# Filler products in front of each piece of maxima in a two-attention, two-mixture block

## The chip, the cores and the metric

The kernel runs on one core of one Trainium2 chip. The metric is the time of one launch in device microseconds (us). Three runs of the kernel before took 1047.31, 1051.62 and 1055.60 us, a median of 1051.62 us. A difference of about 1% (10.5 us) is what a measurement of this kernel tells from no change.

## The reference, cut to what matters

```python
x = x + attention_a(layernorm(x))    # latent projections, 16 heads of 8, rotary part of 32, causal, 1024 tokens, batch 2
x = x + ffn(layernorm(x))            # 8 experts, each takes its top 257 tokens, 128 -> 512 -> 128
x = x + attention_b(layernorm(x))    # 16 heads of 8, causal, the keys in another order
x = x + ffn(layernorm(x))
# either attention:
a = softmax(mask(q @ k.T / scale))   # per head, 1024 x 1024, rows normalised
out = a @ v
```

The softmax is of the exact form: the maximum of every row of scores is subtracted ahead of the exponential. So the kernel computes the scores twice: once with the queries along the partitions to take the maxima, and once with the keys along the partitions, with the negated maximum as one more row of the product, to exponentiate them and multiply them by the values.

## The kernel before, in words

**Stages.** `project_and_attend` is run for attention "a" (latent) and for attention "b", each followed by a feed-forward stage. Each attention first projects (`project_stage`) and then attends (`attention_stage`). The 16 heads of a batch are worked in 4 groups of 4 (`GH`), 8 groups over both batches. A group has two halves of 512 queries: an early one (`c = 0`) and a late one (`c = 1`). `HALVES` is their order: group 0 early, group 0 late, then for every later group late and early. So halves 0, 1 and 2 are (group 0, early), (group 0, late) and (group 1, late).

**Pieces of maxima.** The maxima of a half are taken in pieces, 5 of an early half and 13 of a late one. A piece (`max_piece`, line 905) is a few products into one of two slots of two PSUM banks (`mx`), 1024 columns in all, and in some pieces products that add the causal mask (line 915). VectorE reduces the slot (`take_max`, line 1051) and frees it (`ring_done`). `slot` waits for that before TensorE writes the slot again. When a half has all its maxima, they are joined (late halves), TensorE turns them round (`turn_m`, line 928), VectorE copies the result out (`copy_m`, line 1065), and DMAs issued by SyncE (for half 0 by SyncE and ScalarE) lay them as one row into the queries (`m_rows`, line 750).

**Units of scores.** A unit (`score_unit`, line 950) is one head against one set of keys. ScalarE exponentiates it (line 1032), and after each set of four units some products with the values follow (`values`, line 968). The first unit of a half waits for its row of maxima (`m_in`). TensorE issues everything in the order written out by `tensor`: the table `BESIDE` says which pieces follow which unit. Eleven pieces and turns stand ahead of the first unit: the 5 pieces of half 0, its turn, and the first 5 pieces of half 1. The other 8 pieces of half 1 follow the first 8 units one by one. Then come pieces 0 and 1 of half 2, the turn of half 1, piece 2 of half 2, and from the first unit of half 1 (unit 12) on the other ten pieces of half 2 beside that half's 28 units.

**The queues.** In attention b, `sync` issues on SyncE's queue, right behind the maxima of half 1, the stores of the second batch's queries and keys to memory (lines 620 and 632, 24 DMAs), then the loads of groups 2 and 3 (line 423, 16 DMAs), and only then the maxima of half 2.

**Fillers.** `keep_busy` (line 413) issues products of two constants, 128 rows by 256 columns in bf16, whose result nobody reads. `IDLE` holds their numbers. Before the change, 2 of them follow each of the eleven entries ahead of the first unit, in both attentions, and write to the first score bank `st[0]`. Besides, 36 stand ahead of the projection of b and none ahead of that of a, and 34 (a) and 10 (b) stand between projection and attention. From the first unit on there are none in an attention.

Of the kernel before, what the change touches and what calls it, by code (L numbers as in the profile page):

```python
# [21 lines left out]
P = 128  # L22
# [36 lines left out]
def set_tiles(c, s):  # L59

    out, col = [], 0
    for k in SETS[c][s]:
        first = max(0, k * P - c * CH)
        out.append((k, first, CH - first, col))
        col += CH - first
    return out, col
# [147 lines left out]
def loads_of(kind, n):  # L214

    buffer_groups = range(n % NBUF, n + 1, NBUF)
    return 2 * GH * (n // WAYS + 1) if kind == "b" else 1 + sum(4 if g and rope_load(g) else 2 for g in buffer_groups)


def rope_new(n):  # L220

    return n < NBUF or n // NG != (n - NBUF) // NG
# [7 lines left out]
def rope_copies(n):  # L230

    return 0 if n == 0 or not rope_new(n) else GH - 1 if rope_load(n) else GH
# [169 lines left out]
class Memory:  # L402
    pass


IDLE = {"project": {"a": 0, "b": 36}, "attend": {"a": 34, "b": 10}, "piece": 2, "sum": 8, "turn": [(24, 0, 8, 0), (4, 4, 22, 0)],
        "logits": [(4, 4, 3, 3), (4, 4, 3, 3)]}


def keep_busy(pe, m, to, count):  # L410

    for _ in range(count):
        pe.matmul(to.rearrange("p (a w) -> p a w", a=2), m.ident_b[:, :], m.mask_s[:, :, :], start=True, stop=True,  # L413
                  skip_group_check=True)
# [25 lines left out]
def project_stage(nc, ctx, m, a, kind, sb, loaded):  # L440
# [115 lines left out]
    def tensor(pe):  # L556
        def turn(c):
            for i in range(TPC):
                s.wait_xn(pe, c * TPC + i)
                if c >= 2 and i == 0:  # L560
                    pe.wait_ge(xt_ready, c - 1)
                last = pe.transpose(xn_ps[:, c % 2, i * P:(i + 1) * P], m.xn[:, c * TPC + i, :], m.ident[:, :])
            last.then_inc(turned, 1)

        if latent:
            pe.transpose(one_ps[:, 0:P], m.w_kv[:, :], m.ident[:, :]).then_inc(fuse_mm, 1)
            pe.wait_ge(fused, 1)
            for at, w in ((1, m.w_k), (2, m.w_v)):
                pe.matmul(one_ps[:, at * P:(at + 1) * P], w_kv_t[:, :], w[:, :], start=True, stop=True)
            pe.matmul(one_ps[:, 3 * P:3 * P + 2 * DR], w_kv_t[:, :], m.w_rope[:, 1, :, :].rearrange("p s r -> p (s r)"),  # L570
                      start=True, stop=True).then_inc(fuse_mm, 1)
        keep_busy(pe, m, one_ps[:, 0:2 * P], IDLE["project"][kind])
        turn(0)
# [121 lines left out]
def attention_stage(nc, ctx, m, a, kind, sb, loaded, before, norm):  # L695

    k = f"t{kind}"
    latent = kind == "a"
# [27 lines left out]
    st = [m.banks[:, i, :] for i in range(NST)]  # L726
# [156 lines left out]
    def tensor(pe):  # L883
        def slot(key):

            at = RING[key]
            if at >= 2:
                pe.wait_ge(ring_done, at - 1)
            return mx[at % 2]

        def max_piece(j, x):

            n, c = HALVES[j]
            if x == 0 and j == FIRST[n]:
                pe.wait_ge(loaded[n % (NBUF if latent else WAYS)], 16 * loads_of(kind, n))
                if latent and n == 0:
                    pe.wait_ge(near_rope, 2)
                elif latent and rope_new(n):
                    pe.wait_ge(rope_set, 2 * sum(rope_copies(g) for g in range(n + 1)))
            if latent and (j, x) == (0, 2):  # L900
                pe.wait_ge(far_rope, 2 * (GH - 2))
            to = slot((j, x))
            for products, masks in PIECES[c][x][0]:
                for h, q, k0, w, bank, col in products:
                    last = pe.matmul(to[:, bank, col:col + w], head_rows(q2, n, h, slice(q * P, (q + 1) * P), 0),  # L905
                                     head_rows(k2, n, h, slice(k0, k0 + w), 0), start=True,
                                     stop=k0 + w != (q + 1) * P, skip_group_check=True)
                for bank, col, apart in masks:
                    if apart == 256:
                        out = to[:, bank, :].rearrange("p (a w) -> p a w", a=2)[:, :, col:col + P]  # L910
                    elif apart == P:
                        out = to[:, bank, col:CH].rearrange("p (a w) -> p a w", w=P)
                    else:
                        out = to[:, bank, col:col + P].rearrange("p (a w) -> p a w", w=P)
                    last = pe.matmul(out, m.ident_b[:, :], m.mask_s[:, 0:2 if apart else 1, :],  # L915
                                     start=False, stop=True, skip_group_check=True)
            last.then_inc(ring_ready, 1)

        def turn_m(j):

            n, c = HALVES[j]
            if c == 0:
                pe.wait_ge(ring_done, RING[j, len(PIECES[0]) - 1] + 1)
            else:
                pe.wait_ge(m_joined, late[j])
            to = slot(TURN[j])
            src = mearly[j % 2] if c == 0 else mjoin[j % 2]
            pe.transpose(to[0:GH * TPC, 0, 0:P], src[:, :, :].rearrange("p h q -> p (h q)"),
                         m.ident[:, :]).then_inc(ring_ready, 1)

        def turn_o(i):

            pe.wait_ge(o_copied, i + 1)
            to = slot(("o", i))
            for t in range(TPC):
                last = pe.transpose(to[:, 0, t * P:(t + 1) * P], ot[:, t * P:(t + 1) * P], m.ident[:, :])
            last.then_inc(ring_ready, 1)

        def score_unit(i, v):

            n, c = HALVES[i]
            s, h = divmod(v, GH)
            u = UNIT0[i] + v
            if v == 0:
                pe.wait_ge(m_in[i % 2], m_in_count(i))

            if u >= NST:
                pe.wait_ge(exp_done, u - NST + 1)
            for key, q0, w, col in set_tiles(c, s)[0]:
                last = pe.matmul(st[u % NST][:, col:col + w], head_rows(k2, n, h, slice(key * P, (key + 1) * P), 1),  # L950
                                 head_rows(q2, n, h, slice(c * CH + q0, c * CH + q0 + w), 1),
                                 start=True, stop=True, skip_group_check=True)
            last.then_inc(st_ready, 1)

        def values(i, s):

            n, c = HALVES[i]
            pe.wait_ge(exp_done, UNIT0[i] + (s + 1) * GH)
            if diagonal(c, s):
                pe.wait_ge(masked, masks_before(i, s) + GH)  # L960
            if s == 0:
                pe.wait_ge(v_ready, n + 1)
                if i:

                    pe.wait_ge(o_copied, i)
            for key, q0, w, col in set_tiles(c, s)[0]:
                for h in range(GH):
                    last = pe.matmul(o_ps[VW * h:VW * (h + 1), q0:CH], vg[n % 2][:, key, h, :],  # L968
                                     pt[(SET0[i] + s) % NPT][:, h, col:col + w], start=(key == 0),
                                     stop=(s == len(SETS[c]) - 1), skip_group_check=True)  # L970
            last.then_inc(pv_done, 1)

        def pieces(u):
            for j, x in BESIDE[u]:
                if (j, x) == TURN[j]:
                    turn_m(j)
                else:
                    max_piece(j, x)
                if u < 0:
                    keep_busy(pe, m, st[0][:, 0:2 * P], IDLE["piece"])  # L980

        pe.wait_ge(before.split, before.splits)
        pe.wait_ge(before.copied, NCH)
        keep_busy(pe, m, st[0][:, 0:2 * P], IDLE["attend"][kind])
        pieces(-1)
        for i, (n, c) in enumerate(HALVES):
            for v in range(NU[i]):
                score_unit(i, v)
                for w in (v,) if latent else (v - 1, v)[:v % 2 * 2]:
                    pieces(UNIT0[i] + w)  # L990
                    if w == TURN_O[kind] and i:
                        turn_o(i - 1)
                if v % GH == GH - 1:
                    for s in BURST[kind][c][v // GH]:
                        if s < 0 and i:
                            values(i - 1, s + len(SETS[HALVES[i - 1][1]]))
                        elif s >= 0:
                            values(i, s)
        for s in (-2, -1):
            values(NH2 - 1, s + len(SETS[HALVES[NH2 - 1][1]]))  # L1000
        turn_o(NH2 - 1)
# [155 lines left out]
def feed_forward_stage(nc, ctx, m, a, k, sb, banks, out, norm):  # L1157
# [84 lines left out]
    def tensor(pe):  # L1242
# [89 lines left out]
        for pair in (order[0:2], order[2:4]):  # L1332
            for c in pair:
                keep_busy(pe, m, banks[:, 6, 2 * P:4 * P], IDLE["turn"][k][place[c]])
                turn(c)
            for c in pair:
                keep_busy(pe, m, banks[:, 6, 2 * P:4 * P], IDLE["logits"][k][place[c]])
                logits(c)
# [15 lines left out]
        for c in range(NCH):  # L1354
            if unit_of(CHUNKS - NCH + c) + 23 >= u:
                if not last_layer:
                    keep_busy(pe, m, banks[:, 0, 0:2 * P], IDLE["sum"])
                turn_sum(c)
# [288 lines left out]
```

## Time and profile before

| | |
|---|---|
| median of three runs | 1051.62 us |
| the profiled execution, its own time | 1054.91 us |
| its span, from the first instruction to the last | 1053.2 us |
| TensorE (PE) busy | 968.0 us, 92% of the span |
| VectorE (DVE) busy | 741.0 us, 70% |
| ScalarE (ACT) busy | 694.0 us, 66% |
| mean granted clock of TensorE | 0.964 of full speed |

In the profile, PE is TensorE's matmuls and PEld its weight loads. A time is in us from the start of the span. The first attention lies at about 42 to 330 us, the second at about 571 to 850 us, and a feed-forward stage follows each.

### The profile page before, as it was taken

The numbers are of one execution on the slowest core, as the hardware profiler recorded it, in microseconds if no ns is written. First come the engines' busy times: TensorE is split into PE (matmuls) and PEld (weight loads), VectorE is DVE, ScalarE is ACT, GpSimd is POOL, SyncE is SP. The second block draws the span as 40 slices with busy tenths as digits, with TensorE's granted clock in tenths as the row PEclk, the third lists the DMA queues.
The fourth block names the chain that finished last, engine by engine and source line by source line (L and its number), as shares of the span: only waits on it lengthen the run. The fifth ranks groups of instructions, "written<-read, shape, count | busy, mean of one in ns | idle before, by whom it ended". The sixth has DMA issues, their size and how long they took to land. (4 is left out here: it accounts for less than half of the span.)

```text
span 1053.2 us, 16068 instructions
## 1 busy us (share of the span) xinstructions
PE 968.0 (92%) x5706; PEld 628.2 (60%) x5706; DVE 741.0 (70%) x1310; ACT 694.0 (66%) x1188; POOL 218.5 (21%) x494
## 2 busy tenths in 40 slices
PE   3889999999998999999987999999999889999997
PEld 2555655665545777788864444444444366778886
DVE  4786676776633577689875777777777447678996
ACT  2435666666665699888834266666666759988885
POOL 1342355653332000000005112222322200000000
PEclk9999999999999699999999589999999989999999
DMA  3752343122112011245505270111000021124552
GB/s 90 227 163 48 126 121 91 32 81 71 61 41 81 1 41 41 83 123 157 118 2 138 54 188 15 31 32 32 2 1 2 2 80 39 43 59 121 141 151 52
DMA packets 67727, 78.52 MB, mean 75 GB/s; under 512 B 6512, under 2 KB 55552, under 8 KB 67264
## 3 DMA queue, kind: packets, MB, share of 16 engines
q1 hardware_dynamic: 62432, 72.83, 24.6%
q10 hardware_dynamic: 5216, 4.66, 1.6%
q8 instruction: 46, 0.75, 0.3%
q14 instruction: 33, 0.27, 0.1%
HBM read 53.44 MB, written 22.94 MB: 73 GB/s over the span
## 5 line engine op out<-in xcount | busy, mean ns | idle before, releaser
L1032 ACT ACTIVATE b_pt<-b_banks 128x512 f32<-128x512 f32 (+1 forms) x320 | 154.8, 559 | 102.2 <-PE b_banks L950 102.0
L1307 PE MATMUL f_banks<-f_xr,f_w1r 128*128 128x512 f32 x768 | 191.2, 397 | 0.7 <-ACT f_h L1392 0.7
L1323 PE MATMUL f_banks<-f_hr,f_w2r 128*128 128x512 f32 x768 | 189.0, 394 | 2.5 <-DVE f_hr L1418 2.5
L1392 ACT ACTIVATE f_h<-f_banks,b_t 128x512 f32<-128x512 f32 x256 | 167.1, 681 | 31.0 <-PE f_banks L1307 28.5
L1418 DVE TENSOR_TENSOR f_hr<-f_h,f_hr 128x1024 fp32r<-128x1024 f32 x128 | 156.2, 1223 | 26.9 <-ACT f_hr L1398 25.0
L1307 PEld LDWEIGHTS f_banks<-f_xr,f_w1r 128*128 128x128 f32 x768 | 143.2, 191 | 29.5 <-ACT f_h L1392 1.5
L1323 PEld LDWEIGHTS f_banks<-f_hr,f_w2r 128*128 128x128 f32 x768 | 141.8, 188 | 30.8 <-issue 3.4
L1051 DVE TENSOR_REDUCE a_mlate<-a_banks 128x2 f32<-128x1024 f32 (+3 forms) x120 | 124.8, 1080 | 49.8 <-PE a_banks L905 31.1
L1051 DVE TENSOR_REDUCE b_mlate<-b_banks 128x2 f32<-128x1024 f32 (+3 forms) x120 | 126.2, 1081 | 38.6 <-PE b_banks L915 19.6
L1398 ACT ACTIVATE f_hr<-f_h 128x1024 fp32r<-128x1024 f32 x128 | 136.0, 1063 | 4.1
L1032 ACT ACTIVATE a_q_hl<-a_banks 128x512 f32<-128x512 f32 (+1 forms) x160 | 81.7, 557 | 64.8 <-PE a_banks L950 63.3
L950 PE MATMUL a_banks<-a_q,a_k 121*128 121x512 f32 (+3 forms) x384 | 117.3, 383 | 3.8 <-DMA a_q<-a_mt 2.7
L1032 ACT ACTIVATE a_k_hl<-a_banks 128x512 f32<-128x512 f32 (+1 forms) x160 | 81.7, 558 | 52.4 <-PE a_banks L950 50.8
L905 PE MATMUL a_banks<-a_k,a_q 120*128 120x512 f32 (+3 forms) x384 | 99.3, 361 | 11.3 <-DVE a_mlate L1051 7.7
L950 PE MATMUL b_banks<-b_q,b_k 64*128 64x512 f32 (+3 forms) x384 | 99.6, 424 | 10.3 <-ACT b_pt L1032 8.8
L950 PEld LDWEIGHTS b_banks<-b_q,b_k 64*128 64x128 f32 x384 | 48.1, 191 | 85.6 <-ACT b_pt L1032 55.5
L950 PEld LDWEIGHTS a_banks<-a_q,a_k 121*128 121x128 f32 x384 | 65.2, 191 | 50.1 <-issue 19.3
L905 PE MATMUL b_banks<-b_k,b_q 63*128 63x512 f32 (+3 forms) x384 | 77.9, 396 | 8.2 <-DVE b_mlate L1051 4.5
L968 PE MATMUL b_banks<-b_pt,vg 128*32 128x512 f32 (+3 forms) x768 | 81.7, 517 | 0.0
L905 PEld LDWEIGHTS a_banks<-a_k,a_q 120*128 120x128 f32 x384 | 64.0, 191 | 27.5 <-DVE a_mlate L1051 17.3
L1051 DVE TENSOR_REDUCE b_mearly<-b_banks 128x2 f32<-128x768 f32 (+3 forms) x56 | 49.7, 918 | 23.1 <-PE b_banks L915 22.3
L831 POOL TENSOR_SCALAR_AFFINE_SELECT b_pt<-b_pt 128x128 f32<-128x128 f32 x128 | 36.9, 293 | 137.7 <-ACT b_pt L1032 137.6
(196 smaller groups left out, 1062.0 us busy)
## 6 DMA issues: line engine op xcount, KB each, us to landing
scratch_w<-a_tab SPq DMA_DIRECT2D x16, 512.0 KB, 3.1
f_w1r<-scratch_w SPq DMA_DIRECT2D x16, 512.0 KB, 4.8
f_w2r<-scratch_w SPq DMA_DIRECT2D x16, 512.0 KB, 5.6
v<-scratch_gate SPq DMA_DIRECT2D x32, 256.0 KB, 5.4
xt<-scratch_gate SPq DMA_DIRECT2D x32, 256.0 KB, 5.2
a_rot<-in_w SPq DMA_DIRECT2D x16, 256.0 KB, 3.9
a_q<-scratch_q SPq DMA_DIRECT2D x8, 384.0 KB
a_k<-scratch_k SPq DMA_DIRECT2D x8, 384.0 KB
```

Of the source, the lines that this page charges most:

```text
L831: pool.affine_select(out=block[:, 0:P], in_=block[:, 0:P], compare_op=ALU.is_ge, fill=0.0, base=0, pattern=[[1, P]], channel_multiplier=-1 ...
L905: last = pe.matmul(to[:, bank, col:col + w], head_rows(q2, n, h, slice(q * P, (q + 1) * P), 0), head_rows(k2, n, h, slice(k0, k0 + w), 0), ...
L950: last = pe.matmul(st[u % NST][:, col:col + w], head_rows(k2, n, h, slice(key * P, (key + 1) * P), 1), head_rows(q2, n, h, slice(c * CH + ...
L968: last = pe.matmul(o_ps[VW * h:VW * (h + 1), q0:CH], vg[n % 2][:, key, h, :], pt[(SET0[i] + s) % NPT][:, h, col:col + w], start=(key == 0) ...
L1032: act.activation(pt[at % NPT][:, h, 0:cols], st[u % NST][:, 0:cols], ACT.Exp, scale=scale).then_inc(exp_done, 1)
L1051: last = dve.tensor_reduce(dst, src, AX.X, ALU.max, negate=True)
L1307: last = pe.matmul(h_ps[:, j, :], w1r[e % 2][:, wp, j * P:(j + 1) * P], xr[xp][:, chunk(c)], start=(i == 0), stop=(i == 2))
L1323: last = pe.matmul(y_ps[:, q % 2, :], w2r[e % 2][:, wp, j * P:(j + 1) * P], hr[q % 2][hp][:, j, :], start=(j == 0 and i == 0), stop=(j == ...
L1392: act.activation(h[q % 2][:, j, :], h_ps[:, j, :], ACT.Gelu, bias=m.b1_t[:, e * HB + j:e * HB + j + 1]).then_inc(gelu_done, 1)
L1398: act.activation(hr[q % 2][0][:, j - 1:j + 1, :], h[q % 2][:, j - 1:j + 1, :], ACT.Copy).then_inc(h_high, 1)
L1418: dve.tensor_tensor(hr[q % 2][1][:, first:end, :], h[q % 2][:, first:end, :], hr[q % 2][0][:, first:end, :].bitcast(F32), ALU.subtract).th ...
```

## The change

Fillers no longer follow the entries ahead of the first unit. Instead they stand ahead of the products of a piece, behind the wait for its slot, and write to that slot, where the piece's products then write over them. In attention a that is done for the 5 pieces of half 0, with 2 fillers each. In attention b it is done for the pieces of halves 0, 1 and 2, with 3 fillers each. The turns have none.

```diff
-IDLE = {"project": {"a": 0, "b": 36}, "attend": {"a": 34, "b": 10}, "piece": 2, "sum": 8, "turn": [(24, 0, 8, 0), (4, 4, 22, 0)],
+IDLE = {"project": {"a": 0, "b": 36}, "attend": {"a": 34, "b": 10}, "piece": {"a": 2, "b": 3}, "sum": 8, "turn": [(24, 0, 8, 0), (4, 4, 22, 0)],
...
             to = slot((j, x))
+            if j == 0 or j <= 2 and not latent:
+                keep_busy(pe, m, to[:, 0, 0:2 * P], IDLE["piece"][kind])
             for products, masks in PIECES[c][x][0]:
...
                     max_piece(j, x)
-                if u < 0:
-                    keep_busy(pe, m, st[0][:, 0:2 * P], IDLE["piece"])
```

## Rows read from the trace of the kernel before

**Rows 1.** The page: TensorE's busy time, and its granted clock in 40 slices.
```profile
PE 968.0 (92%) x5706; PEld 628.2 (60%) x5706; DVE 741.0 (70%) x1310; ACT 694.0 (66%) x1188; POOL 218.5 (21%) x494
PEclk9999999999999699999999589999999989999999
```

**Rows 2.** Groups by line, shapes apart: line, engine, operation, count | busy us, mean ns | idle before.
```profile
L413 PE MATMUL b_banks<-mask_s,ident_b 128*128 128x256 bf16 x68 | 12.7, 333 | 1.8 <-PEq L1541 1.0 <-ACT v L553 0.8
```

**Rows 3.** Windows of 5 us: busy PE, PEld, DVE, ACT, POOL, then the granted clock, DMA.
```profile
575.00:580.00 5.00, 3.44 (x25) 1.65 (x23) 4.53 (x6) 0.00 (x0) 0.00 (x0) 0.90 0.87 211
585.00:590.00 5.00, 5.00 (x22) 2.26 (x20) 4.53 (x6) 1.09 (x2) 0.58 (x2) 0.50 0.25 74
...
605.00:610.00 5.00, 4.73 (x28) 2.20 (x28) 3.49 (x3) 2.17 (x4) 0.00 (x0) 0.50 0.94 222
610.00:615.00 5.00, 5.00 (x31) 2.36 (x32) 3.00 (x3) 3.23 (x7) 0.00 (x0) 0.68 0.87 203
```

**Rows 4.** Timeline, start of attention b: start us, duration, engine, line, operands [idle before].
```profile
572.54 0.50 PE L905 MATMUL b_banks<-b_k,b_q 63*128 63x384 f32 x4
...
579.34 0.38 PE L928 MATMUL b_banks<-ident,b_mearly 128*16 128x128 f32 x1 [1.22 <-DVE b_mearly L1051]
...
579.51 0.64 PE L413 MATMUL b_banks<-mask_s,ident_b 128*128 128x256 bf16 x2
...
584.52 0.80 PE L905 MATMUL b_banks<-b_k,b_q 63*128 63x512 f32 x2
...
585.24 0.61 PE L413 MATMUL b_banks<-mask_s,ident_b 128*128 128x256 bf16 x2
...
585.78 0.79 PE L905 MATMUL b_banks<-b_k,b_q 63*128 63x512 f32 x2
```

**Rows 5.** Timeline of PE: the turns of halves 0 and 1 in attention a.
```profile
52.41 0.28 PE L928 MATMUL a_banks<-ident,a_mearly 128*16 128x128 f32 x1 [1.10 <-DVE a_mearly L1051]
...
70.25 0.27 PE L928 MATMUL a_banks<-ident,a_mjoin 128*16 128x128 f32 x1 [0.53 <-DVE a_mlate L1051]
```

**Rows 6.** The same in attention b: turn of half 1, first units of halves 1 to 3.
```profile
600.00 0.38 PE L928 MATMUL b_banks<-ident,b_mjoin 128*16 128x128 f32 x1
...
604.60 0.80 PE L950 MATMUL b_banks<-b_q,b_k 64*128 64x512 f32 x2 [0.49 <-DMA b_q<-b_mt]
...
629.74 0.51 PE L950 MATMUL b_banks<-b_q,b_k 64*128 64x512 f32 x2
...
651.21 0.50 PE L950 MATMUL b_banks<-b_q,b_k 64*128 64x512 f32 x2
```

**Rows 7.** Windows by stage of attention b, columns as in rows 3.
```profile
579.30:600.00 20.70, 19.30 (x78) 9.06 (x78) 17.37 (x19) 6.28 (x11) 3.36 (x10) 0.50 0.20 55
...
604.60:629.70 25.10, 23.76 (x151) 10.58 (x151) 17.88 (x21) 14.41 (x29) 3.93 (x12) 0.83 0.73 188
```

**Rows 8.** Timeline of VectorE in attention a: the 13 pieces of half 1.
```profile
53.42 15.13 DVE L1051 TENSOR_REDUCE a_mlate<-a_banks 128x2 f32<-128x1024 f32 x15 [0.41 <-PE a_banks L905]
```

**Rows 9.** Timeline of PE in attention a: fillers, then the first piece.
```profile
44.30 1.04 PE L413 MATMUL a_banks<-mask_s,ident_b 128*128 128x256 bf16 x8
45.24 0.78 PE L905 MATMUL a_banks<-a_k,a_q 120*128 120x384 f32 x4
```

**Rows 10.** Timeline of SyncE's DMA issues in attention b.
```profile
601.07 2.45 SPq L750 DMA_DIRECT2D b_q<-b_mt  x4
...
623.66 1.59 SPq L423 DMA_DIRECT2D b_q<-scratch_q  x4
625.88 2.78 SPq L750 DMA_DIRECT2D b_q<-b_mt  x4
```

**Rows 11.** Windows of 2 us in attention a, columns as in rows 3.
```profile
72.00:74.00 2.00, 0.31 (x3) 0.03 (x2) 1.29 (x2) 0.00 (x0) 0.00 (x0) 0.96 0.01 3
74.00:76.00 2.00, 1.03 (x3) 0.84 (x4) 0.00 (x0) 0.20 (x1) 0.00 (x0) 0.50 0.40 99
...
78.00:80.00 2.00, 2.00 (x8) 0.99 (x11) 1.80 (x2) 1.38 (x3) 0.00 (x0) 0.50 0.93 142
80.00:82.00 2.00, 2.00 (x27) 0.98 (x20) 0.44 (x1) 0.24 (x1) 0.00 (x0) 0.83 0.67 90
```

## The prediction, made before the change was run

> **What bounds the kernel now.** I read the page first. TensorE is busy for 92% of the span, and its granted clock dips in a few slices, the longest of them near slices 22 to 23, which is the start of the second attention [rows 1]. The windows come next. From 575 to 580 the clock goes from 1.00 towards 0.50 (2.4 to 1.2 GHz) while PE is busy for 3.44 of 5 us. It is 0.50 from there on and comes back inside 610 to 615 (0.68) [rows 3], so the low stretch is about 34 us long. Over it VectorE works almost as much as TensorE: 17.37 us against 19.30 in the 20.70 us between the turns of halves 0 and 1 [rows 7]. The reader should see two different bounds. At full clock VectorE's reductions set the pace of the pieces: in attention a 13 pieces took 15.13 us without a gap, 1.16 us each [rows 8]. At half clock TensorE does: in attention b a piece and its two fillers take 1.26 us (584.52 to 585.78), and a masked one more [rows 4].
>
> **What goes and comes.** Attention a: 22 fillers go, 10 come. Attention b: 22 go, and 3 x (5 + 13 + 13) = 93 come, so line 413 will have 68 - 22 + 93 = 139 products there where it has 68 [rows 2]. A filler takes 0.94 / 8 = 0.12 us from start to start at full clock [rows 9], and 0.54 / 2 = 0.27 us at half clock (585.24 to 585.78) [rows 4]. Three are 0.35 or 0.81 us. They stand behind the wait for the slot, so they lie between VectorE's freeing of a slot and the products that it reads next, and all later units, values and pieces queue behind them on TensorE.
>
> **Does the clock stay up?** It fell behind the one hole of this stretch: TensorE waited 1.22 us for the last reductions of half 0 before the turn at 579.34 [rows 4]. The change leaves this hole (no filler goes there) but puts 3 fillers in place of 2 around it, and then 3 more ahead of each piece. I take it that the clock stays at full, or falls only briefly. That is the weakest step.
>
> **The sum, clock up.**
> 1. First piece of b: its products waited for nothing but the load and the fillers before (at 572.54) [rows 4]; now three more stand ahead of them: +0.35 us. It is fully on the path, since VectorE has nothing else.
> 2. Turn of half 0 to turn of half 1. In b this takes 600.00 - 579.34 = 20.66 us at half clock [rows 4, 6]. The same pieces in a took 70.25 - 52.41 = 17.84 us at full clock [rows 5]. That is -2.82 us. The fillers' part: a slot is filled while VectorE takes 1.16 us for the other one. Products of a plain piece are visible 0.5 us after their start [rows 4], with 0.35 us ahead that is under 1.16: hidden. The 5 masked pieces of the 13 are nearer to the limit; a filler group can cost each between 0 and 0.35 us (0 to 1.75), and I take 0.1 each, +0.5, as most of the 0.3 us that is left over should hide them. One filler more than in a ahead of the first piece: +0.12. Sum -2.2 us. If VectorE loses its cover, by waits on the slot's products, this term is what goes.
> 3. Turn of half 1 to the first unit of half 1: 4.60 us [rows 6]. TensorE does little in it and waits for the rows of maxima by DMA: 0.
> 4. Half 1, from its first unit to that of half 2: 629.74 - 604.60 = 25.14 us, a third of it at half clock (mean 0.83) [rows 6, 7]. The next late half takes 651.21 - 629.74 = 21.47 us at full clock [rows 6]: -3.67 us. Ten pieces with three fillers come in, TensorE being busy for 23.76 of 25.10 us [rows 7], so hardly anything hides them: +3.5 us. Sum -0.2 us. There is a floor too: SyncE's queue works from 601.07 through the stores and loads to 625.25 (623.66 + 1.59), and issues the maxima of half 2 at 625.88 [rows 10]. Half 1 can shrink by no more than this 0.6 us, whatever TensorE does.
> 5. Attention a: the first piece gets 2 fillers ahead of it, +0.23 us, since there they follow on one another without a wait [rows 9]. The piece behind the turn loses its 2, -0.2 us, as VectorE waited 0.41 us for it [rows 8]. The other ten that go lie under VectorE's pace: 0. Sum 0; bounds -0.3 and +0.3 us.
>
> Total 0.35 - 2.2 - 0.2 + 0 = about -2 us. Against the profiled execution's own 1054.91 us (1.7 us more than its span) that is 1052.9. That execution was 3.3 us above the median of the runs shown, so for the median I take 1051.62 - 2, **1050 us**.
>
> **Rivals.**
> *B: the clock falls for a short time.* In attention a it fell behind a hole (PE busy 0.31 us in 72 to 74) and came back inside 80 to 82, with TensorE full, some 7 us later [rows 11]. The same in b, at 579 or in the hole behind the turn of half 1, means four or five pieces at 1.26 + 0.27 = 1.5 us or more instead of 1.16 us, about +2 us: 1051.6 us. For it: the hole stays, and the gap behind the turn of half 1 is the place where a fell.
> *C: the clock falls and stays down as before (the slower side).* For it: from 585 to 590 TensorE was busy for 5.00 of 5 us and the clock stayed at 0.50 [rows 3], so a fuller TensorE is no sure cure; the fillers then only cost. From the turn of half 0 to that of half 1: ten pieces with three more fillers at half clock (8 of half 1, two of half 2), 8.1 us, and five with one more (3 for 2), 1.35 us, less the 1.4 us in which TensorE is idle there [rows 7]: +8 us. Behind it, one piece and four of half 1's stretch at half clock, +4, six at full clock, +2.1, less 1.3 us idle [rows 7]: about +5. With step 1: +13 us, about 1064 us. It decides from the turn of half 0 at 579: if the clock is 0.50 from there for over about 15 us, the change loses. The Trainium skill, "TensorE: Matmul & The Clock Gate", section "What's actually happening", has it that the throttled state is the default and that activity releases it; by that rule TensorE as full as here should have been released before 590, and filling it further should not be needed. The row above disagrees with it taken as busy time. Against C: a filler uses all 128 rows of the array, a score product 63 [rows 2, 4], so the fillers raise what the array does more than they raise the busy time.
> *D: attention a loses its clock.* With 12 fillers fewer, it could fall at the first turn there (hole of 1.10 us at 52.41 [rows 5]), where it didn't. Three to four pieces at half clock then cost 0.3 to 0.5 us each: +1.5 us, 1051.5 with the rest as forecast.
> *E: the gain is taken by the queue.* Should half 1's own pieces go quicker than thought, SyncE's 24 us of issues keep its length: that is inside the forecast's range.
> The same page, section "Part 4: PE-mode transpose", says that a transpose doesn't count as busy for the clock in the way that a product does. By it the turns, which lose their fillers, are bare spots, and B gets likelier. No row here separates it.
>
> **How the numbers follow.** Forecast, with D's small price within: 0.50. B: 0.27. C: 0.14. The rest, 0.09, is for other clocks elsewhere: each low stretch of the trace may be longer or shorter in another run, and the three runs differ by 8.3 us. The low end: without any cost of the fillers the gain is 2.8 + 0.6 = 3.4 us, and with a median that falls 3 us lower by such chance 1045. The high end: B with the upper bound of step 2 (+1.25) and D (+1.5) is 1054; reaching into C, of which a half-long low stretch gives about 1058, I stop at 1061. Faster by over 1% (below 1041.1) has no mechanism: 0.03. Slower by over 1% (above 1062.1) is most of C: 0.13. Within 1%: 0.84.
>
> **What would show it.** Right: granted clock 1.00 from 575 to about 600, 139 fillers in b, 13 reductions of half 1 in 15.2 to 16 us, turn to turn 18.4 us, then first unit of half 1 to first unit of half 2 in about 25 us, with SyncE's issue of the maxima of half 2 within 1 us of the end of its loads. Step 2's price shows as waits of VectorE for lines 905 and 915. Wrong: clock 0.50 for over 15 us behind 579, VectorE waiting at each piece, a new low stretch in a before 70 us, or a half 1 that is longer than 26 us.

## The result: 0.44% slower, where 0.2% faster was forecast

Over 20 runs each the changed kernel took 1054.69 us (median; 1050.61 to 1067.64) and the kernel before 1051.08 us (1044.71 to 1056.63). The ratio is 1.0044, with a 95% interval from 1.0023 to 1.0064: about 4.6 us slower. The ratios here and below leave out runs that are over 1.5% above the fastest of their own kernel (1 of the change's 20, 2 of 116 of the kernel before, up to 4 of 12 in an experiment, with 1332.38 us in e5 and 1941.13 us in e6 among them), and the profile of e1 is of such a run, whose long low stretch, 34.1 us from 833.1 on, lies behind the stages read here. The time lies within the forecast's range and within 1%, but the forecast's direction, 2 us faster, was wrong.

The profiled execution of the changed kernel had a span of 1058.7 us, where the one before had 1053.2. The page's line of the clock, and the group of fillers in b, 139 as counted ahead (the columns are those of [rows 1, 2]):

```profile
PEclk9989999999999899999999699999999999999999
```
```profile
L413 PE MATMUL b_banks<-mask_s,ident_b 128*128 128x256 bf16 x139 | 24.4, 307 | 4.6 <-DVE b_mlate L1051 1.4 <-PEq L1541 1.0 <-ACT v L553 0.8
```

The same windows as in [rows 3], of the changed kernel. The lines from 903 to 978 stand two higher there, so that 905, 915, 928 and 950 are now 907, 917, 930 and 952, and 413 and 1051 are the same:

```profile
575.00:580.00 5.00, 3.88 (x29) 1.87 (x27) 4.56 (x7) 0.00 (x0) 0.00 (x0) 1.00 0.90 217
580.00:585.00 5.00, 4.03 (x18) 1.99 (x20) 3.28 (x4) 1.28 (x1) 0.00 (x0) 0.65 0.47 109
585.00:590.00 5.00, 4.98 (x21) 2.12 (x19) 3.90 (x5) 0.60 (x2) 0.00 (x0) 0.50 0.51 157
590.00:595.00 5.00, 5.00 (x19) 2.07 (x18) 2.66 (x3) 1.57 (x3) 1.10 (x4) 0.50 0.00 0
595.00:600.00 5.00, 5.00 (x25) 2.59 (x23) 2.79 (x3) 1.08 (x2) 0.88 (x3) 0.50 0.00 0
600.00:605.00 5.00, 4.46 (x25) 2.22 (x23) 4.55 (x6) 1.75 (x4) 1.38 (x4) 0.81 0.00 0
```

The clock fell all the same, at 581.5, and was back at 601.9: the low stretch is 20.5 us where it was 34.1. It came back earlier, but this pair of executions doesn't show that the fillers did that: with b as before it was once low for 20.5 us too (e2), and without any filler beside b's pieces for 23.9 us (e3). And from 590 to 600 TensorE is busy for 10 of 10 us and VectorE for only 5.45: TensorE had become the bound of the pieces. By stage, with the same columns, turn to turn and half 1 (before [rows 7]):

```profile
581.00:606.40 25.40, 24.83 (x110) 11.64 (x110) 17.66 (x19) 6.29 (x11) 3.36 (x10) 0.60 0.16 45
...
611.20:636.80 25.60, 24.86 (x181) 11.09 (x181) 17.84 (x21) 14.68 (x29) 3.94 (x12) 1.00 0.72 184
```

VectorE's work is what it was (17.66 us, before 17.37); TensorE's went from 19.30 to 24.83 us. TensorE's timeline shows the two prices of a group of three. At 573.11 and 575.76 it is at full clock, at 587.40 at half:

```profile
573.11 0.50 PE L413 MATMUL b_banks<-mask_s,ident_b 128*128 128x256 bf16 x3 [0.47 <-DMA b_k<-scratch_k]
573.54 0.50 PE L907 MATMUL b_banks<-b_k,b_q 63*128 63x384 f32 x4
...
574.63 0.50 PE L907 MATMUL b_banks<-b_k,b_q 63*128 63x512 f32 x2
575.06 0.29 PE L917 MATMUL b_banks<-mask_s,ident_b 128*128 128x128 bf16 x2
...
575.76 0.50 PE L413 MATMUL b_banks<-mask_s,ident_b 128*128 128x256 bf16 x3 [0.41 <-DVE b_mearly L1051]
...
580.97 0.28 PE L930 MATMUL b_banks<-ident,b_mearly 128*16 128x128 f32 x1 [1.32 <-DVE b_mearly L1051]
...
587.40 0.82 PE L413 MATMUL b_banks<-mask_s,ident_b 128*128 128x256 bf16 x3
588.14 0.79 PE L907 MATMUL b_banks<-b_k,b_q 63*128 63x512 f32 x2
```

Three fillers push the products back by 0.43 us at full clock (573.11 to 573.54) and by 0.74 at half (587.40 to 588.14). And VectorE's timeline shows who pays. It took the seven reductions of half 0 without a gap before (the first line below, of the kernel before); now it waits in between, and in half 1 at nearly each piece (the others, of the changed kernel):

```profile
573.41 5.88 DVE L1051 TENSOR_REDUCE b_mearly<-b_banks 128x2 f32<-128x768 f32 x7 [2.36 <-PE b_banks L915]
```
```profile
574.41 2.42 DVE L1051 TENSOR_REDUCE b_mearly<-b_banks 128x2 f32<-128x768 f32 x3 [3.33 <-PE b_banks L917]
577.05 2.42 DVE L1051 TENSOR_REDUCE b_mearly<-b_banks 128x2 f32<-128x768 f32 x3 [0.22 <-PE b_banks L917]
579.69 1.23 DVE L1051 TENSOR_REDUCE b_mearly<-b_banks 128x4 f32<-128x1024 f32 x1 [0.22 <-PE b_banks L917]
...
595.11 1.23 DVE L1051 TENSOR_REDUCE b_mlate<-b_banks 128x2 f32<-128x1024 f32 x1 [0.98 <-PE b_banks L907]
...
599.66 2.60 DVE L1051 TENSOR_REDUCE b_mlate<-b_banks 128x2 f32<-128x768 f32 x3 [1.52 <-PE b_banks L917]
```

Where the two profiled executions part, stage by stage (starts of the first piece, the turns and the first units, as in [rows 4 to 6]):

| stage | before | changed | difference |
|---|---|---|---|
| start to first piece of a | 45.24 | 46.38 | +1.1 |
| first piece of a to first unit of its half 1 | 29.73 | 33.09 | +3.4 |
| from there to the first piece of b | 497.57 | 494.07 | -3.5 |
| b: first piece to turn of half 0 | 6.80 | 7.43 | +0.6 |
| b: turn of half 0 to turn of half 1 | 20.66 | 25.48 | +4.8 |
| b: turn of half 1 to first unit of half 1 | 4.60 | 4.72 | +0.1 |
| b: half 1, to first unit of half 2 | 25.14 | 25.67 | +0.5 |
| from there to the end | 423.46 | 421.86 | -1.6 |

The sum is +5.5 us. The first piece is timed by its products, so the fillers ahead of it lie in the row before: in the first row for a, in the third for b (0.43 us there). Apart from them the -3.5 and -1.6 lie where the code is the same. In the first of them one low stretch was 10.2 us long where it was 17.1. So single executions differ by as much as the change is worth, and the experiments had to read stages, not totals.

### The profile page after: what moved, and what is told of

It reads as the page before. It is cut to its first block and busy times, and to the rows that moved or that the text cites. A ratio compares the mean times of both kernels' runs of the same rounds, so it can differ in the third digit from the quotient of the medians.

```text
span 1058.7 us, 16186 instructions
## 1 busy us (share of the span) xinstructions
PE 969.9 (92%) x5765; PEld 628.4 (59%) x5765; DVE 741.9 (70%) x1310; ACT 694.4 (66%) x1188; POOL 218.9 (21%) x494
## 5 line engine op out<-in xcount | busy, mean ns | idle before, releaser
L952 PE MATMUL b_banks<-b_q,b_k 64*128 64x512 f32 (+3 forms) x384 | 97.0, 417 | 10.6 <-ACT b_pt L1032 8.2
L970 PE MATMUL b_banks<-b_pt,vg 128*32 128x512 f32 (+3 forms) x768 | 79.0, 500 | 0.0
L1051 DVE TENSOR_REDUCE b_mearly<-b_banks 128x2 f32<-128x768 f32 (+3 forms) x56 | 49.9, 918 | 23.9 <-PE b_banks L917 23.3
```

The source lines that it names most:

```text
L1051: last = dve.tensor_reduce(dst, src, AX.X, ALU.max, negate=True)
```

## The experiments

All were timed in five rounds beside the kernel before; "a" and "b" are the two attentions. (on e1) means that an edit is shown against the kernel of e1. The table gives the ratio and, from the one profiled execution of each, the stages of b, with the us of low clock in turn to turn.

| kernel | ratio (95%) | first piece to turn 0 | turn 0 to turn 1 (low) | turn 1 to half 2 |
|---|---|---|---|---|
| before | 1 | 6.80 | 20.66 (20.7) | 29.74 |
| the change | 1.0044 (1.0023, 1.0064) | 7.43 | 25.48 (20.5) | 30.39 |
| e1 a old, b new | 1.0031 (1.0000, 1.0063) | 7.44 | 24.39 (17.1) | 30.38 |
| e2 a new, b old | 1.0020 (0.9997, 1.0043) | 6.80 | 17.93 (8.1) | 29.41 |
| e3 none in b | 1.0011 (0.9986, 1.0036) | 6.81 | 19.33 (19.3) | 29.13 |
| e4 b's first ten pieces | 1.0029 (1.0007, 1.0051) | 7.44 | 20.63 (18.4) | 29.46 |
| e5 six per piece | 1.0072 (1.0042, 1.0101) | 8.10 | 21.81 (0) | 33.21 |
| e6 off the chain, pairs split | 0.9994 (0.9956, 1.0032) | 6.79 | 20.24 (3.4) | 30.29 |
| e7 holes filled | 0.9968 (0.9940, 0.9997) | 6.80 | 18.18 (8.8) | 29.36 |
| e8 half 2 alone | 1.0005 (0.9976, 1.0035) | 6.79 | 19.72 (10.7) | 31.09 |
| e9 holes alone | 1.0000 (0.9968, 1.0032) | 7.10 | 18.97 (15.6) | 29.45 |
| e10 change and holes | 1.0028 (1.0003, 1.0053) | 7.43 | 18.84 (0) | 30.58 |
| e11 holes, 8 more in a | 1.0008 (0.9976, 1.0041) | 6.80 | 17.98 (8.3) | 30.11 |
| e12 holes, off the chain | 0.9992 (0.9964, 1.0019) | 6.80 | 17.83 (0) | 29.65 |

**e1: a as before, b as changed.**

```diff
-            if j == 0 or j <= 2 and not latent:
+            if j <= 2 and not latent:
...
+                if u < 0 and latent:
+                    keep_busy(pe, m, st[0][:, 0:2 * P], IDLE["piece"][kind])
```

> Attention a as before the change, attention b as changed. Theory P (path): three fillers behind the wait for a slot lengthen the chain from VectorE's freeing of the slot to its next reduction, so in b the stretch from the start of the 10 fillers to the turn of half 0 stays near 9.3 us (before 7.98), turn of half 0 to turn of half 1 stays over 22 us at whatever clock (before 20.66), half 1 is 25 to 26 us; total +3 to +6 us over before. Rival A (attention a): the loss comes from the 12 fillers that a lost and its low clock behind 55 us; then this kernel is within 1 us of before, and a's turn to turn is back at 17.8 us. Rival C (clock): if the clock stays up in b, turn to turn is 18.5 us and the kernel is 2 us faster.

Ratio 1.0031. The stretches of b are 7.44, 24.39 and 30.38 us, near those of the change (turn to turn is 1.1 us shorter, with the clock low for 17.1 us in place of 20.5), and a's turn to turn is back at 17.86 us. Theory P holds in the stages: b is slower with a as before. How much of the loss is b's the interval, 0 to 6.6 us, doesn't say.

**e2: a as changed, b as before.**

```diff
-            if j == 0 or j <= 2 and not latent:
+            if j == 0 and latent:
...
+                if u < 0 and not latent:
+                    keep_busy(pe, m, st[0][:, 0:2 * P], 2)
```

> Attention a as changed, attention b as before the change. Theory P: a has half as many fillers on its chain (2 ahead of 5 pieces), so +0.5 us there, and with the clock that falls at the first turn of a up to +4 us in some runs; total +0.5 to +2 us over before. Rival A: the whole +4.6 us is here, with a low stretch of 7 us or more that begins between 50 and 60 us and a turn to turn of 20 to 21 us in a (before 17.84).

Ratio 1.0020, not clear of 1. In a, the clock fell at 52.8, for 3.4 us. The windows of a, in e2:

```profile
52.00:54.00 2.00, 1.13 (x4) 0.89 (x5) 1.09 (x2) 0.00 (x0) 1.83 (x3) 0.71 1.00 387
54.00:56.00 2.00, 1.77 (x7) 0.98 (x6) 1.86 (x2) 0.00 (x0) 2.00 (x3) 0.50 0.72 279
```

In the changed kernel it fell at 55.8 for 10.2 us, with a's turn to turn at 20.94 us; in e2 that is 18.48 us, before it was 17.84. In the seven profiles in which a is as before (before, e1, e3 to e6, e8) it never fell between 46 and 73. So with the hole ahead of a's turn open, the 12 fillers that a lost seem to have held it there, in seven profiles against two; with the hole filled it stayed up without them in e10 (turn to turn 17.63 us), but not in e12, where it fell at 61.2. What their loss costs is less clear. In e4 a is as before and its clock was up throughout, and still turn to turn took 19.20 us, since the first unit of half 0 came late by DMA. That wait, in e4 and then in the changed kernel:

```profile
60.48 0.50 PE L952 MATMUL a_banks<-a_q,a_k 121*128 121x512 f32 x1 [1.56 <-DMA a_q<-a_mt]
```
```profile
61.32 0.79 PE L952 MATMUL a_banks<-a_q,a_k 121*128 121x512 f32 x1 [1.06 <-DMA a_q<-a_mt]
```

So of the 3.1 us that a's turn to turn is longer in the changed kernel, a part comes in other executions without a filler changed and without a low clock. Rival A, that all of the loss is here, is not excluded by e2's ratio, whose interval reaches 1.0043; it falls by e1, where b's turn to turn is 3.7 us longer with a as before, and by e4 and e5, which leave a as before and are slower by intervals above 1.

By accident e2 gives more: its b is the old one, but in this execution the clock stayed up for 9.8 us behind the turn of half 0. Turn to turn was 17.93 us against the 20.66 of [rows 4, 6], so in this stage, with the old fillers, the low clock costs 2.7 us.

**e3: no fillers beside the pieces of b.**

```diff
-"piece": {"a": 2, "b": 3}
+"piece": {"a": 2, "b": 0}
```

(on e1)

> Attention a as before, and no fillers at all beside the pieces of b. Theory P: without fillers each piece at half clock is 0.5 us shorter on TensorE, so turn to turn in b is 18.5 to 20 us even though the clock falls at 579 or before and stays low for 25 us or more; total -1 to +1 us. Rival C: without fillers the clock stays low longer than 34 us, and the kernel is 3 us or more slower than before, which would say that fillers pay.

Ratio 1.0011 (0.9986 to 1.0036). The clock was low for 23.9 us, not longer than before, so rival C's condition was not met. Turn to turn in e3, all of it at half clock:

```profile
575.70:595.10 19.40, 16.61 (x66) 7.89 (x66) 17.22 (x19) 6.28 (x11) 3.36 (x10) 0.50 0.21 60
```

19.33 us with the clock down throughout, where the old fillers made it 20.66 and full clock makes it 17.9. So 1.3 us of the old 20.66 were the fillers themselves, and the low clock as such cost only 1.4 us in this stage, since VectorE is busy for 17.22 of 19.40 us whatever TensorE's clock. The slower clock was hidden for the most part.

**e4: three fillers ahead of the first ten pieces of b alone.**

```diff
-            if j <= 2 and not latent:
+            if not latent and (j, x) < (1, 5):
```

(on e1)

> Attention a as before; in b three fillers ahead of each of the 5 pieces of half 0 and the first 5 of half 1, none ahead of the others. Theory P: start to turn of half 0 as in the change (9.3 us), the later pieces at VectorE's pace if the clock is up and 1.2 to 1.4 us if it is low; turn to turn 19.5 to 22 us, half 1 23 to 25 us; total 0 to +2 us over before, 3 us under the change. Rival C: the fillers beside the units are what brought the clock back at 601.6; without them it stays low to 613 or later and this kernel is no faster than the change.

7.44, then 20.63 us, at low clock from 584.9 on, for 30.7 us. Ratio 1.0029 (1.0007 to 1.0051), which is about 3 us over before where theory P had 0 to 2. Against the change's 25.48 the eight pieces beside units and two of half 2 save 4.9 us of turn to turn, 0.49 us each. Rival C has this execution for it, with a low stretch nearly as long as before, and e3 against it, with 23.9 us and no fillers at all. The stages of b don't explain the ratio: they add up to 0.3 us more than in the profile before, the fillers ahead of b's first piece to 0.4, and the longer wait in a, shown under e2, to 1.4 us. Where the rest lies is open.

**e5: six in place of three.**

```diff
-"piece": {"a": 2, "b": 3}
+"piece": {"a": 2, "b": 6}
```

(on e1)

> Attention a as before; in b six fillers in place of three ahead of each of the 31 pieces. Theory P (the fillers lie on the chain from the freed slot to the next reduction): 0.35 us more for each of the early pieces, so first product to turn of half 0 goes from 7.4 to about 8.8 us (no fillers: 6.8), turn to turn from 24 to 25.5 up to 29 to 33 us at half clock, or 23 to 25 us at full clock; the turn of half 1 to that of half 2 from 25.3 to 28 us or more; total 8 to 14 us over before. Rival C (clock): six of them keep TensorE so full that the clock stays up or returns within 7 us, turn to turn is 22 us or less, and the kernel is no slower than with three.

Ratio 1.0072 (1.0042 to 1.0101). Here the clock did stay up. Turn to turn, then the turn of half 1 to the first unit of half 2, in e5:

```profile
582.80:604.60 21.80, 21.33 (x156) 12.76 (x156) 17.73 (x19) 6.28 (x11) 3.36 (x10) 1.00 0.13 38
604.60:637.80 33.20, 30.78 (x235) 14.90 (x234) 20.53 (x25) 15.38 (x31) 4.50 (x14) 1.00 0.56 143
```

The full clock bought 2.7 us and the fillers took 3.9 of turn to turn, 1.3 ahead of it and 3.5 behind it. Theory P had the first two stages higher (8.8, and 23 to 25 us at full clock) and the total too (8 to 14 us, measured 7.6), and turn to turn is even 3.7 us shorter than with three fillers at half clock; but rival C's kernel that is no slower than with three is not there. This is the sharpest case for theory P: clock 1.00 all along b, and the slowest kernel of all.

**e6: the same 93 fillers, off the chain.** (on e1)

```diff
-            if j <= 2 and not latent:
-                keep_busy(pe, m, to[:, 0, 0:2 * P], IDLE["piece"][kind])
...
             if u >= NST:
                 pe.wait_ge(exp_done, u - NST + 1)
+            if not latent:
+                keep_busy(pe, m, st[u % NST][:, 0:2 * P],
+                          IDLE["piece"][kind] * sum(j <= 2 and (j, x) != TURN[j] for j, x in BESIDE[u]))
...
+                    if u < 0 and not latent:
+                        keep_busy(pe, m, st[0][:, 0:2 * P], IDLE["piece"][kind])
                     max_piece(j, x)
```

> Attention a as before; in b the same 93 fillers, but off the slots' chain: ahead of the wait for the slot (into the first score bank) in the first ten pieces, and ahead of the unit of scores that a piece follows (into that unit's bank) in the others. Theory P: TensorE does them while it would wait for VectorE, so first product to turn of half 0 is 6.8 us as without fillers, and the pieces at full clock keep VectorE's 1.16 us; turn to turn 18 us at full clock and 22 to 24 us at half clock, where TensorE itself is the bound; total 0 to +3 us over before. Rival Q (count): it is the fillers' own time on TensorE and not their place that costs; then turn to turn and total are as in the change, 24 to 25.5 us and +4 us.

Ratio 0.9994 (0.9956 to 1.0032). 6.79 us to the turn of half 0, as without fillers: there the place is the whole price. But 20.24 us of turn to turn, with a low clock for 3.4 us only. A likely reason is in TensorE's timeline of e6: units that ran two at a time now run singly, with a group between them.

```profile
585.03 0.50 PE L953 MATMUL b_banks<-b_q,b_k 64*128 64x512 f32 x1
585.46 0.50 PE L413 MATMUL b_banks<-mask_s,ident_b 128*128 128x256 bf16 x3
585.89 0.50 PE L953 MATMUL b_banks<-b_q,b_k 64*128 64x512 f32 x1
```

A single unit takes 0.43 us here (585.03 to 585.46), as long as a pair does between products of 128 rows (574.63 to 575.06, above). The place was mine to choose badly; e12 does it again without that. It also fills the holes, so what the split costs by itself is not shown.

**e7: the holes filled.**

```diff
+                    if j == 0:
+                        keep_busy(pe, m, st[0][:, 0:2 * P], IDLE["hole"][kind][0])     # 9
                     turn_m(j)
...
+                if i == 1:
+                    pe.wait_ge(exp_done, u - NST + 1)
+                    keep_busy(pe, m, st[u % NST][:, 0:2 * P], IDLE["hole"][kind][1])   # a: 18, b: 8
                 pe.wait_ge(m_in[i % 2], m_in_count(i))
```

(on the kernel before; the comments give the numbers)

> The kernel before, with fillers also in the two holes: 9 ahead of the turn of half 0, and ahead of the first unit of half 1, before its wait for the maxima, 18 in a and 8 in b. Theory H: the clock falls behind the holes (73.8 and 579.0 before); filled, it stays up, b's turn to turn is 18 us, a loses its low stretch of 7 us, and the kernel is 3 to 5 us faster than before. Rival: the clock falls all the same within 15 us of the turn of half 0, since the pieces between leave the array idle often enough, and the kernel is within 1.5 us of before.

Ratio 0.9968 (0.9940 to 0.9997), median 1049.61 us: the only kernel whose interval lies below 1, by 3.4 us (0.3 to 6.3). The clock fell not at the turn (578.1) but at 587.5, so theory H's clock is not there in full, and turn to turn was 18.18 us. The low stretch of a behind 74 is gone; one of 3.4 us came at 61.8 (61.4 in the text of e11 below), behind another wait for DMA, and a's turn to turn was 20.06 us.

**e8: three fillers ahead of half 2's pieces alone.**

```diff
-            if j <= 2 and not latent:
+            if j == 2 and not latent:
```

(on e1, with 2 fillers behind each of b's eleven entries as before)

> The kernel before, with three fillers ahead of the 13 pieces of half 2 in b alone. Theory P with the queue's floor: two of these pieces stand ahead of the turn of half 1, so turn to turn grows by 0.7 to 1.6 us; from there to the turn of half 2 TensorE's extra 3.5 us are partly covered by SyncE's 24.2 to 24.5 us of issues, so 25.0 to 25.6 us where it was 24.5 to 24.9; total +1 to +2 us over before. Rival: no cover, turn of half 1 to turn of half 2 is 28 us and the total +4 us.

Ratio 1.0005 (0.9976 to 1.0035), and 31.09 us from the turn of half 1 to half 2 (before 29.74), partly at low clock. TensorE was busy for 25.56 of 26.30 us of half 1. So this half pays 1.35 us for 3.5 us of fillers, and that with the clock low for 6.4 us of it where it was low for 13.2 before. From turn to turn of halves 1 and 2 it is 26.29 us: more than theory P's 25.6, less than the rival's 28.

**e9: fillers in the holes and nowhere beside the pieces.**

```diff
-"piece": {"a": 2, "b": 2}
+"piece": {"a": 0, "b": 0}
```

(on e7)

> No fillers beside the pieces in either attention; only those in the two holes (9 ahead of the turn of half 0, 18 in a and 8 in b ahead of the first unit of half 1, before its wait). Theory H (filled holes are what pays): as fast as with both kinds, 2 to 4 us under before, with a mean clock of at least 0.975. Rival: the fillers between the pieces are needed to keep the clock; without them it falls in the stretch ahead of the first unit, and the kernel is within 1 us of before.

Ratio 1.0000 (0.9968 to 1.0032), and the clock fell at 59.6 in a and at 585.3, ahead of the turn, in b. The rival holds: the holes alone don't hold the clock, for which the old fillers between the pieces have their use. That they save time isn't shown, since the intervals of e7 and e9 overlap.

**e10: the change, with the holes filled.**

The edit is that of e7, on the changed kernel.

> The change with the holes filled as well. Theory P (fillers on the chain cost whatever the clock): the clock stays up over the turn of half 0 and turn to turn in b is 19.5 to 21.5 us, start to turn 7.4 us from the first product, half 1 25.5 to 26 us; total 2 to 5 us over the kernel with holes filled and fillers as before, so -1 to +2 us against before. Rival C (the change only lacked the clock): with the clock up turn to turn is 18 to 18.5 us and the kernel is 3 us or more under before.

The clock stayed up, and this is the case that I had forecast. VectorE's timeline of e10:

```profile
584.61 2.36 DVE L1056 TENSOR_REDUCE b_mlate<-b_banks 128x2 f32<-128x1024 f32 x2 [0.48 <-PE b_banks L907]
587.19 4.68 DVE L1056 TENSOR_REDUCE b_mlate<-b_banks 128x2 f32<-128x768 f32 x5 [0.23 <-PE b_banks L917]
592.10 3.69 DVE L1056 TENSOR_REDUCE b_mlate<-b_banks 128x4 f32<-128x1024 f32 x3 [0.22 <-PE b_banks L917]
596.19 4.69 DVE L1056 TENSOR_REDUCE b_mlate<-b_banks 128x2 f32<-128x768 f32 x5 [0.40 <-PE b_banks L917]
```

Turn to turn 18.84 us (forecast 18.4; between theory P's 19.5 and rival C's 18.5), and still the ratio is 1.0028 (1.0003 to 1.0053). Rival C falls: with the clock up the change does not pay either. Its three stages of b add up to 56.85 us, though, and those of b as before to 57.20 in one execution and 54.14 in another (e2), so the size of the loss can't be read from one profile of each.

**e11: as e7, and 8 more in a, ahead of the first unit's wait.**

```diff
+                if i == 0 and latent:
+                    keep_busy(pe, m, st[0][:, 0:2 * P], 8)
                 if i == 1:
```

> The kernel with both holes filled and fillers between the pieces as before the change, and 8 more in a ahead of the first unit's wait for its maxima, where TensorE waited 1.5 us in that kernel and the clock fell at 61.4. Theory H: the low stretch of 3.4 us there goes; 3 to 4 us under before. Rival: that fall costs nothing, since VectorE sets the pace there; no faster than without the 8, by less than 0.5 us.

The low stretch at 61 went, and b's turn to turn was 17.98 us, but the ratio is 1.0008 (0.9976 to 1.0041). In a, turn to turn still took 19.65 us at full clock (20.06 in e7), with a wait of 1.13 us for the DMA of the maxima, which is as the rival has it: the fall cost little there. The intervals of e7 and e11 overlap, and e11 did not repeat e7's gain, so that gain is not settled.

**e12: as e10, with the fillers off the chain and the pairs kept.**

```diff
-            if j == 0 or j <= 2 and not latent:
-                keep_busy(pe, m, to[:, 0, 0:2 * P], IDLE["piece"][kind])
...
+            if not latent and v % 2 == 0:
+                keep_busy(pe, m, st[u % NST][:, 0:2 * P],
+                          IDLE["piece"][kind] * sum(j <= 2 and (j, x) != TURN[j] for j, x in BESIDE[u] + BESIDE[u + 1]))
...
+                    if u < 0 and (j == 0 or not latent):
+                        keep_busy(pe, m, st[0][:, 0:2 * P], IDLE["piece"][kind])
                     max_piece(j, x)
```

> The change with the holes filled, and with the same numbers of fillers moved off the slots' chain: ahead of the wait for the slot in the pieces ahead of the first unit, and in b ahead of each pair of units of scores for the pieces that follow the pair, so that the pair is not split. Theory P (place): at full clock first product to turn of half 0 is 6.8 us (on the chain 7.4), and turn to turn 17.9 to 18.3 us (on the chain 18.8). Rival Q (count): 6.8 us too, but turn to turn 18.8 us or more, since TensorE's own work per piece is then as long as VectorE's. Both: from the turn of half 1 to the first unit of half 2 30 to 31 us, as on the chain, since TensorE is full there.

VectorE's timeline of e12, to be read against that of e10:

```profile
574.13 5.88 DVE L1059 TENSOR_REDUCE b_mearly<-b_banks 128x2 f32<-128x768 f32 x7 [2.69 <-PE b_banks L915]
...
581.15 10.41 DVE L1059 TENSOR_REDUCE b_mlate<-b_banks 128x2 f32<-128x1024 f32 x10 [0.49 <-PE b_banks L905]
591.73 4.68 DVE L1059 TENSOR_REDUCE b_mlate<-b_banks 128x2 f32<-128x768 f32 x5 [0.17 <-PE b_banks L915]
```

The gaps are gone but for 0.17 us: 6.80 and 17.83 us, against 7.43 and 18.84 on the chain, with the same 93 fillers and the clock at 1.00 in both. Rival Q falls. Ratio 0.9992 (0.9964 to 1.0019), so even off the chain three per piece gain nothing that is clear of the noise. At full clock the place costs 0.6 + 1.0 us up to the turn of half 1, and 0.9 us behind it (30.58 against 29.65), where I had expected no difference. These are differences of one execution each; the intervals of the two ratios overlap.

## Why the prediction was wrong, step by step

**Does the clock stay up?** This step failed, the one that I had called the weakest. In the change the clock fell 0.5 us behind the turn of half 0, in e1 2.1 us behind it, and stayed low for 20.5 and 17.1 us, not for the 7 us of rival B. In the kernel before it had fallen at 579.0, inside the hole and not behind it. The hole ahead of the turn was still there, 1.32 us now. In b, only kernels with six per piece (e5) or with three per piece and the hole filled (e10, e12) kept full clock over the turn of half 0 and on to that of half 1; the hole filled and the old two were not enough (e7, e11), and with the hole open and the old two it once fell only 9.8 us behind the turn (e2).

**Step 2, the 2.8 us for the clock** were read rightly from attention a (17.84; e2 gave 17.93 and e12 17.83 in b itself), but I took them as the price of the clock alone. e3 shows that half of it was the price of the old fillers at half clock. And the fillers' part was read for full clock only. At half clock a group is 0.74 us between a freed slot and its products, and the cover, VectorE's 1.16 us per piece, is gone: 25.48 us where I had put 18.4. At full clock it would have been 18.84 (e10), so there the term was nearly right. The fillers on the chain cost 1.0 us there (18.84 against 17.83 in e12) where I had 0.6. This is rival C in kind, with its point of decision, over 15 us of low clock, met. Its own size was too high: it said +8 for turn to turn, and the runs show +4.8. It had the whole stage at half clock, and the last 4.5 us were at full; and it priced three fillers at 0.81 us, where a group took 0.74.

**Step 1** had +0.35. The group costs 0.43 us, and six cost 0.74 (575.35 to 576.09 in e5): about 0.1 us each and 0.1 us more per group, which I had spread over the eight of [rows 9]. I take that to be the weight load of the product behind it, which starts only with that product, at 573.54; no run separates it. I had also overlooked that all five pieces of half 0 are masked, so that the chain from freed slot to reduction is longer than VectorE's work on the other slot: another +0.63, the same in the change, e1, e4 and e10.

**Steps 3 and 4** had 0 and -0.2; they measured +0.1 and +0.5, at full clock. The floor is right and decides. SyncE's timeline of the changed kernel, then of e3:

```profile
607.64 2.44 SPq L750 DMA_DIRECT2D b_q<-b_mt  x4
...
630.04 1.60 SPq L423 DMA_DIRECT2D b_q<-scratch_q  x4
632.98 2.78 SPq L750 DMA_DIRECT2D b_q<-b_mt  x4
```
```profile
596.15 2.45 SPq L750 DMA_DIRECT2D b_q<-b_mt  x4
...
618.64 1.59 SPq L423 DMA_DIRECT2D b_q<-scratch_q  x4
620.34 2.77 SPq L750 DMA_DIRECT2D b_q<-b_mt  x4
```

In the change the queue is free at 631.64 and issues at 632.98, so TensorE is 1.3 us late. In e3, without a filler, it issues the moment it is free, and half 2 begins 29.13 us behind the turn of half 1, against 29.74 before. So nothing on TensorE can make this stretch more than 0.6 us shorter than before. The clock that the change has there from 601.9 on could only carry the fillers, 3.5 us in half 1, and did not carry all of them: half 1 took 25.67 us, not 25.0.

**Step 5** had 0, and rival D +1.5. D came true in its condition: a lost its clock at 55.8 in the change and at 52.8 in e2. In e2 turn to turn was 0.6 us longer for it. In the change it was 3.1 us longer, with a wait of 1.06 us for the DMA of maxima; since e4 shows +1.4 with such a wait and the clock up, D's own price stays open. I had given it no more than a place within the forecast.

**The total.** Over the runs that enter the ratios, as far as their clock was recorded, the mean granted clock was 0.980 with the change (19 runs) and 0.975 before (114 runs beside the experiments). A line through each kernel's runs falls by 5.2 us (before) to 6.8 us (the change) per hundredth of clock, and at a clock of 0.980 it gives 1056.0 us with the change and 1050.0 before. By this estimate the fillers cost about 6 us and the higher clock gives about 3 us back (0.5 hundredths at 6 us): 3 us, against the measured 4.6 (2.4 to 6.7). This is a reading of the spread, on several chips, and no experiment by itself; that the higher clock comes from the fillers is not shown by it. That the time lies within the forecast's range is luck as far as the sum goes: the range had been drawn to reach into rival C, and it is a loss of C's kind that came. How the loss divides between a and b stays open within the intervals of e1 and e2.

## What to carry to other kernels

A filler belongs where TensorE would stand still anyway: ahead of a wait, not between the wait and the work that it gates. Even there none here is shown to pay: e7's gain did not come again. Ask first what the low clock costs in that stage. Where another engine sets the pace, or a DMA queue sets the length, it costs little, and the fillers at half clock cost more than it does. Price a filler at the clock that it will meet, and don't put it between two matmuls that now run side by side. And look at more than one execution before a stage's change is put down to an edit: a wait for DMA or a low stretch moved here with no edit near it.

## What was not expected of the hardware

- A TensorE that is busy without a gap is not enough for the clock to come back. In the change it was busy for 10 of 10 us from 590 to 600 at 0.50. With six fillers per piece (e5) it never fell there.
- The same code in b meets other clocks in other executions. With b as before, the clock fell at 579.0 in one profile (34.1 us low) and at 592.1 in another (20.5 us low), and the stretch from b's first piece to half 2 took 57.20 and 54.14 us.
- Score products of two heads run side by side. Two of 63 rows by 512 columns (line 905) take 0.24 us together, from 617.65 to the next product at 617.89 in the kernel before. Ahead of products of 128 rows such a pair takes 0.43 us (574.63 to 575.06 in the change), and a single product of 64 rows takes 0.43 us too (585.03 to 585.46 in e6).
- The DMA of the maxima in a lands sooner in some executions than in others. The first unit of half 0 stood 5.4 us behind the turn before and in e1, and 7.2 us behind it in e4, with the same code of a and the clock up in all three.
